# Taylor-softmax attention and an FP6 feed-forward layer on one core: attention in units of two quads by 256 tokens, its rest in 64-row tiles, and the stream normalised on ScalarE

## The reference

```python
x = x + _layernorm(attention(_layernorm(x)))     # x: 16 sequences x 512 tokens x 256
x = x + _layernorm(ffn(_layernorm(x)))
# attention: layer norm with weights, q, k, v of 16 heads of 16; rope on q and k
qk = einsum('bhkd,bhqd->bhkq', q, k) * scale
t = 1.0 + qk + 0.5 * qk * qk
wv = einsum('bhkq,bhqd->bhkd', t / sum(t, -1), v);  return wv @ w_o
# ffn: input and weight rounded to a 6-bit grid in blocks of 32, then x @ w.T + bias
```

## Time and profile before

| | |
|---|---|
| median of 3 runs | 645.59 us (644.71 to 646.18) |
| the profiled execution | 645.33 us, its span 643.7 us |
| PE (TensorE) busy | 615.6 us, 96% |
| VectorE (DVE) busy | 594.8 us, 92% |
| ScalarE (ACT) busy | 530.3 us, 82% |
| GpSimd (POOL) busy | 449.9 us, 70% |
| granted TensorE clock, mean | 0.994 |

### The profile page before, as it was taken

One profiled execution on the slowest core, in us unless ns is written; L12 is line 12 of the kernel. 1 busy time (PEld: TensorE's weight loads), 2 busy tenths in 40 slices (PEclk: granted clock), 3 DMA queues, 4 the chain that ended last, 5 costly groups with the idle time before them and its releaser, 6 DMA issues. The chain is left out here.

```text
span 643.7 us, 20804 instructions
## 1 busy us (share of the span) xinstructions
PE 615.6 (96%) x6660; PEld 459.2 (71%) x6660; DVE 594.8 (92%) x1489; ACT 530.3 (82%) x1448; POOL 449.9 (70%) x785
## 2 busy tenths in 40 slices
PE   8889999899999999999999999999999999999974
PEld 6766667676686777777777777767777766778763
DVE  6999989899899999999999999999999999987796
ACT  4358788788798897989888888978888888999984
POOL 3565476567777778787877777766877777765454
PEclk9999999999999999999999999999999999999997
DMA  7101022222223332332313222223223211230101
GB/s 247 34 3 42 20 78 57 44 68 61 53 74 85 80 81 75 76 87 62 74 53 85 85 72 80 68 58 111 51 71 90 76 39 42 75 85 19 67 27 50
DMA packets 52362, 43.53 MB, mean 68 GB/s; under 512 B 7200, under 2 KB 48544, under 8 KB 52256
## 3 DMA queue, kind: packets, MB, share of 16 engines
q1 hardware_dynamic: 51440, 41.42, 23.9%
q10 hardware_dynamic: 816, 0.79, 0.4%
HBM read 18.65 MB, written 8.39 MB: 42 GB/s over the span
## 5 line engine op out<-in xcount | busy, mean ns | idle before, releaser
L1168 ACT ACTIVATE feat<-ps_f 128x512 f32<-128x512 f32 x256 | 144.5, 599 | 4.9 <-PE ps_f L852 4.3
L691 DVE TENSOR_TENSOR kf<-kf 128x896 f32<-128x896 f32 (+1 forms) x128 | 132.0, 1033 | 1.8
L852 PE MATMUL ps_f<-qT,selr 128*128 128x512 f32 x320 | 122.1, 435 | 1.6 <-ACT qT L1236 1.3
L691 POOL TENSOR_TENSOR kf<-kf 128x224 f32<-128x224 f32 x64 | 76.5, 1195 | 13.3 <-DVE kf L1515 13.0
L1015 PEld LDWEIGHTS ps_mt<-kf,vp 128*32 128x32 f32 x2048 | 63.7, 109 | 29.7 <-issue 28.2
L1015 PE MATMUL ps_mt<-kf,vp 128*32 128x153 f32 x2048 | 79.0, 294 | 0.8 <-DVE kf L691 0.8
L1725 POOL TENSOR_TENSOR qsp<-kf,qsp 128x256 fp32r<-128x256 f32 x64 | 57.8, 903 | 9.8 <-ACT qsp L1259 9.6
L852 PEld LDWEIGHTS ps_f<-qT,selr 128*128 128x128 f32 x320 | 52.8, 190 | 14.9 <-issue 11.0
L913 PE MATMUL ps_o<-feat,main 120*32 120x512 f32 x448 | 59.7, 604 | 0.0
L916 PE MATMUL ps_o<-feat,rm 128*32 128x512 f32 x448 | 58.6, 593 | 0.0
L1737 POOL TENSOR_TENSOR kf<-kf 128x128 f32<-128x128 f32 x64 | 38.2, 596 | 25.6 <-DVE kf L1508 25.5
(11 more groups left out here) (199 smaller groups left out, 1887.4 us busy)
## 6 DMA issues: line engine op xcount, KB each, us to landing
xc<-L_attn_x SPq DMA_DIRECT2D x16, 512.0 KB, 4.5
result<-fin SPq DMA_DIRECT2D x64, 128.0 KB, 2.0
xa<-L_attn_x SPq DMA_DIRECT2D x15, 512.0 KB, 4.3
heads_out<-osb SPq DMA_DIRECT2D x224, 32.0 KB, 2.0
shares<-sums SPq DMA_DIRECT2D x112, 64.0 KB
sums<-osb SPq DMA_DIRECT2D x224, 2.0 KB
wkqv<-L_attn_w_kv ACTq DMA_DIRECT2D x2, 256.0 KB, 4.5
xa<-L_attn_x SPq DMA_DIRECT2D x1, 384.0 KB, 5.8
```

The costliest lines, as they stand in the source:

```text
L691: return eng.tensor_tensor(dims(row, F_MAIN, [[FW, heads], [HD, NR - 1], [1, HD]]), dims(row, F_LIN, [[FW, heads], [0, NR - 1], [1, HD]]), ...
L852: pe.matmul(ps_f[i % 2][:, :], selr[:, i], queries, start=True, stop=True).then_inc(sel_done, 1)
L1168: act.activation(feat[:, p2, i], ps_f[i % 2][:, :], ACT.Square).then_inc(squared, 1)
```

## The change

It has three parts and a new order.

**Units.** In the body a unit is now two quads (p and p+2) by 256 tokens, still 56 of them. Its result goes into two banks: quad p to ps_o, quad p+2 to ps_f[1], so that ps_f[1] is shared with the odd selects. `select_1` and `select_3` wait until the last unit's copy has freed it (f_copied), `attend` until the squares of the odd selects are done. The moving operands of `attend` are 256 columns wide, and there are 16 matmuls in a unit instead of 8. `copy_quad` is two activations of 128x256 in the body instead of one of 128x512. `rm` holds on rows 0 to 63 the rest of quad p and on rows 64 to 127 that of quad p+2; in the second half of `attend` each matmul takes 64 rows and 32 columns, and the two row halves write to different banks. In the last two sequences a unit is still 4 quads by 128 tokens, with the rest in 64-row tiles as well. `fold_kq` puts the columns of w_q in an order to suit (8 matmuls of 2x64 columns and 4 of 256 for 4 of 512, once), and `rest_matrix` and `copy_rest` write the new layout of `rm` with as many instructions as before. `move_quad` has as many DMAs of as many bytes. A unit needs only the queries of its own half of the sequence.

**Normalisation.** `normalise_x` moves from VectorE to ScalarE (z = rs * x + centre_x, scale and bias both read from memory), and POOL gets a new stage `shift_x`, which computes centre_x, 64 of each.

**Order.** All tables of `ORDER` are new (one line of them is shown below); `constant` and `rest_terms` on VectorE are each cut into two stages, and there are 16 idle fills at the start for 10, and 44 idle matmuls for 32 in all.

```diff
-"load_stream": ((0, 1, 6, 11, 20, 32,), (-24,), (76, 87, 98, 108, 119,)),
...
+"load_stream": ((0, 2, 7, 9, 19, 33, 38, 55, 62, 76, 92, 102, 110, 119,), (), ()),
...
-IDLE = {"fill": (4, 4, 4, 4, 4, 6, 6, 7, 7, 9), "drain": ()}
+IDLE = {"fill": (1, 1, 1, 1, 2, 3, 6, 6, 6, 6, 11, 11, 11, 16, 16, 23,), "drain": ()}
...
-rm = sb("rm", [P, 2, NQ, P])
+rm = sb("rm", [P, 2, CH, HQ, VW])
...
+def attend_bank(e):
+
+    return ps_f[1] if e else ps_o
...
+        sp.wait_ge(f_copied, t.n)
         sp.wait_ge(o_copied, t.n)
-        for part in range(NT):
-            sp.dma_start(sums[part * H + HQ * quad:part * H + HQ * (quad + 1)],
-                         osb[HD:P:VW, par, quad, part * P:(part + 1) * P]).then_inc(sums_in, 16)
+        half, p = quad // 2, quad % 2
+        for part in (2 * half, 2 * half + 1):
+            for qd in (p, p + 2):
+                sp.dma_start(sums[part * H + HQ * qd:part * H + HQ * (qd + 1)],
+                             osb[HD:P:VW, par, qd, part * P:(part + 1) * P]).then_inc(sums_in, 16)
         for h in range(HQ):
-            row = HD * (HQ * (quad % 2) + h)
-            sp.dma_start(heads_out[row:row + HD, par, quad // 2], osb[VW * h:VW * h + HD, par, quad]).then_inc(heads_in[par], 16)
+            row = HD * (HQ * p + h)
+            sp.dma_start(heads_out[row:row + HD, par, :, half * 2 * P:(half + 1) * 2 * P],
+                         osb[VW * h:VW * h + HD, par, p:NQ:2, half * 2 * P:(half + 1) * 2 * P]).then_inc(heads_in[par], 16)
...
+    def attend_bank_is_free():
+
+        wait(pe, f_copied, issued["attend"])
...
-            pe.wait_ge(qT_copied, t.n if t.n > BODY else NT * (t.seq + 1))
+            pe.wait_ge(qT_copied, t.n if t.n > BODY else NT * t.seq + 2 * (quad // 2 + 1))
         wait(pe, squared, CHUNKS * n + i - 1 if i else CHUNKS * n)
-        queries = qT[:, par, :, quad * P:(quad + 1) * P] if t.n > BODY else qT[:, par, quad]
+        if i % 2:
+            attend_bank_is_free()
+        half, p = quad // 2, quad % 2
+        queries = (qT[:, par, :, quad * P:(quad + 1) * P] if t.n > BODY
+                   else qT[:, par, 2 * p:2 * p + 2, half * 2 * P:(half + 1) * 2 * P])
         pe.matmul(ps_f[i % 2][:, :], selr[:, i], queries, start=True, stop=True).then_inc(sel_done, 1)
...
+    def feature_bank_is_free():
+
+        if issued["select_1"]:
+            pe.wait_ge(squared, CHUNKS * (issued["select_1"] - 1) + 2)
+        if issued["select_3"]:
+            pe.wait_ge(squared, CHUNKS * (issued["select_3"] - 1) + 4)
...
     def attend(t):
-        par, p2, quad = t.par, t.two, t.tile
-        n = t.n - 1
+        par, p2 = t.par, t.two
+
+        def part(p):
+            return slice(p * P, (p + 1) * P) if t.n > BODY else slice(0, 2 * P)
+
+        def tokens(p, j):
+            g = 2 * p + j // 2
+            return slice(g * P, (g + 1) * P) if t.n > BODY else slice(j // 2 * 2 * P, (j // 2 + 1) * 2 * P)
         wait(pe, o_copied, issued["attend"])
         pe.wait_ge(rm_copied, t.seq + 1)
-        pe.wait_ge(squared, CHUNKS * (n + 1))
-        if t.n > BODY:
-            for qd in range(NQ):
-                part = slice(qd * P, (qd + 1) * P)
-                for h in range(HQ):
-                    pe.matmul(ps_o[VW * h:VW * (h + 1), part], main[0:NP, par, qd, VW * h:VW * (h + 1)], feat[0:NP, p2, h, part],
-                              start=qd == 0, stop=False, skip_group_check=True)
-            for qd in range(NQ):
-                part = slice(qd * P, (qd + 1) * P)
-                for h in range(HQ):
-                    mm = pe.matmul(ps_o[VW * h:VW * (h + 1), part], rm[:, par, qd, VW * h:VW * (h + 1)], feat[:, p2, HQ, part],
-                                   start=False, stop=True, skip_group_check=True)
-            mm.then_inc(quad_done, 1)
-            return
-        for h in range(HQ):
-            pe.matmul(ps_o[VW * h:VW * (h + 1), :], main[0:NP, par, quad, VW * h:VW * (h + 1)], feat[0:NP, p2, h],
-                      start=True, stop=False, skip_group_check=True)
-        for h in range(HQ):
-            mm = pe.matmul(ps_o[VW * h:VW * (h + 1), :], rm[:, par, quad, VW * h:VW * (h + 1)], feat[:, p2, HQ],
-                           start=False, stop=True, skip_group_check=True)
+        pe.wait_ge(squared, CHUNKS * t.n)
+        feature_bank_is_free()
+        pairs = range(CH) if t.n > BODY else [t.tile % 2]
+        for p in pairs:
+            for e in range(2):
+                for j in range(HQ):
+                    pe.matmul(attend_bank(e)[VW * j:VW * (j + 1), part(p)], main[0:NP, par, p + 2 * e, VW * j:VW * (j + 1)],
+                              feat[0:NP, p2, 2 * e + j % 2, tokens(p, j)], start=p == pairs[0], stop=False, skip_group_check=True)
+        for p in pairs:
+            for j in range(HQ):
+                for e in range(2):
+                    rows = slice(e * P // 2, (e + 1) * P // 2)
+                    mm = pe.matmul(attend_bank(e)[VW * j:VW * (j + 1), part(p)], rm[rows, par, p, j],
+                                   feat[rows, p2, HQ, tokens(p, j)], start=False, stop=True, skip_group_check=True)
+                    if p == pairs[-1] and j == HQ - 1 and e == 0:
+                        mm.then_inc(first_done, 1)
...
+    def normalise_x(t):
+        act.wait_ge(x_centred, t.n)
+        wait(act, zT_done, t.n - 2)
+        act.activation(z[:, t.two, 0:D - 1], xa[:, t.par, t.tile, 0:D - 1], ACT.Identity,
+                       bias=centre_x[:, t.two:t.two + 1], scale=rs["x"][:, t.two:t.two + 1]).then_inc(z_ready, 1)
...
+        act.wait_ge(first_done, t.n)
...
+        half, p = quad // 2, quad % 2
         if t.n > BODY:
-            for qd in range(NQ):
-                ins = act.activation(osb[:, par, qd, quad * P:(quad + 1) * P], ps_o[:, qd * P:(qd + 1) * P], ACT.Identity,
+            for qd in (2, 3, 0, 1):
+                ins = act.activation(osb[:, par, qd, quad * P:(quad + 1) * P],
+                                     attend_bank(qd // 2)[:, qd % 2 * P:(qd % 2 + 1) * P], ACT.Identity,
                                      bias=cb[:, par, qd:qd + 1])
+                if qd == 3:
+                    ins.then_inc(f_copied, 1)
             ins.then_inc(o_copied, 1)
             return
-        act.activation(osb[:, par, quad], ps_o[:, :], ACT.Identity, bias=cb[:, par, quad:quad + 1]).then_inc(o_copied, 1)
+        part = slice(half * 2 * P, (half + 1) * 2 * P)
+        act.activation(osb[:, par, p + 2, part], attend_bank(1)[:, 0:2 * P], ACT.Identity,
+                       bias=cb[:, par, p + 2:p + 3]).then_inc(f_copied, 1)
+        act.activation(osb[:, par, p, part], attend_bank(0)[:, 0:2 * P], ACT.Identity,
+                       bias=cb[:, par, p:p + 1]).then_inc(o_copied, 1)
...
+        wait(dve, x_centred, t.n - 2)
         dve.bn_aggr(mv[:, t.two], st[:, t.two]).then_inc(means, 1)
-
-    def normalise_x(t):
-        dve.wait_ge(rstd["x"], t.n)
-        wait(dve, zT_done, t.n - 2)
-        dve.tensor_scalar(z[:, t.two, 0:D - 1], xa[:, t.par, t.tile, 0:D - 1], mv[:, t.two, 0:1], rs["x"][:, t.two:t.two + 1],
-                          ALU.subtract, ALU.mult).then_inc(z_ready, 1)
-
...
+    def sum_linear(t):
+
+        dve.wait_ge(mt_copied, t.seq + 1)
+        wait(dve, cb_ready, t.seq)
+        dve.tensor_reduce(lins[:], mts[:, :, F_LIN:NF], AX.X, ALU.add).then_inc(lins_done, 1)
+
     def constant(t):
-
-        dve.wait_ge(mt_copied, t.seq + 1)
-        dve.tensor_reduce(lins[:], mts[:, :, F_LIN:NF], AX.X, ALU.add).then_inc(lins_done, 1)
         dve.wait_ge(lins_done, t.seq + 1)
...
+    def scale_terms(t):
...
+    def rest_terms(t):
...
+        wait(pool, z_ready, t.n - 2)
         inverse_root("x", t)
+
+    def shift_x(t):
+
+        pool.wait_ge(rstd["x"], t.n)
+        wait(pool, z_ready, t.n - 2)
+        pool.tensor_scalar(centre_x[:, t.two:t.two + 1], mv[:, t.two, 0:1], rs["x"][:, t.two:t.two + 1], -1.0,
+                           ALU.mult, ALU.mult).then_inc(x_centred, 1)
```

541 lines of the change are left out of this document (283 added, 258 removed), and 97 rows, old and new, of the table ORDER.

## The result

The change takes 658.65 us (median of 4 runs, 657.05 to 659.64) against 645.46 for the kernel before (4 runs, 644.71 to 646.18): a ratio of 1.0202, 95% interval 1.0179 to 1.0226. It is 13 us slower; the forecast was 631.5, 14 us faster. The profiled execution has a span of 656.9 us, 13.2 above the 643.7 of before.

What follows compares the result with a forecast made beforehand. PE was taken to set the pace, VectorE just behind. From 645.33 us: -10.0 for 120 to 560 us, -2.8 for the units before, -1.4 for the last units, +0.4 at the start, giving 631.5; range 620 to 642.

Steps and rivals of the forecast that it cites:

- (a): Second half of attend (the rest) on PE: eight 64-row tiles run side by side, 0.87 us becomes 0.435 a unit.
- rival 4: The rest on PE: the two row halves take turns, so it keeps its 0.87 us; 655 us, chance 0.05.
- the 5 foretold: Sign on PE: odd selects' waits for the copy of the shared bank total under 5 us.
- (b): Between the halves of attend on PE: the new change of tile shape adds 0.10 us a unit, bounds 0 and 0.14.
- Rival 2: Shape change within attend on PE: a full drain costs 0.18 us instead of 0.10; 636 us, chance 0.16.
- I give it 10.3 now: PE's gaps from 120 to 560 us: 10.3 us beside 419.7 busy, so the stretch takes 430 instead of 440.
- 411.9 fits into 440: ScalarE from 120 to 560 us: 0.69 us more a unit raises its busy time from 379.43 to 411.9 us.
- rival 3: ScalarE from 120 to 560 us: its in-order waits stay, 40 us of gaps; 653.5 us, chance 0.06.
- The first 120 us: Start of the kernel: a change there of more than 3 us would show the prediction wrong.

Runs made afterwards that it cites:

- The load: Kernel before, plus a 128x128 copy on ScalarE that nobody reads behind each of the 56 unit copies: 3.8 us more; the same was also added to the change.
- copy_vector: The change, with the first of each unit's two copies (from the second bank) on VectorE instead of ScalarE: 675.13 us.
- z_pool_new: The change, with the stream's normalisation on POOL in place of the shift, and four buffers for z: 672.52 us.
- z_pool_old: The kernel before in its own order, with only the stream's normalisation moved from VectorE to POOL: 679.55 us.
- z_old_order: The kernel before, old units and old order, with only the normalisation moved to ScalarE and its shift on POOL: 661.53 us.
- start_list: The change, with the heads of the TensorE, VectorE and POOL lists put nearer to those of the kernel before: 665.51 us.
- shape_price: The change, plus ten rounds each of several mixes of matmul shapes behind the last attend, with no waits: 0.14 to 0.20 us per shape change.

## Why the prediction was wrong

**Right.** PE was the engine with the highest price (0.79 of each us), though not the only bound. The rest takes 0.43 us in eight tiles, as (a) had it: rival 4 is out. The odd selects wait 1.3 us for the copy of their bank by the page, but 4.9 over the whole run when the starts are taken, just under the 5 foretold. The prices of the pieces on ScalarE were near or too high: z 0.52 us from start to start in the mean, the two copies 0.37 each, 0.74 against 0.60 where I added 0.20; its busy time rose by 32 instead of 44 us.

**The shape change (b), mis-sized.** I took 0.10 us for one change, from rows of full size against strips. It is 0.14 into the 64-row tiles and 0.16 out of them: with the changes that fell away 9.0 us in all instead of 6.4. `attend` gives 0.18 a unit instead of 0.31. Rival 2, the drain at 0.18, was near in size but had one change for two. This is some 3 of the 27 us.

**The step that failed: "PE had 5.75 us of gaps ... I give it 10.3 now. This number is chosen, not read."** The page's gaps of PE after are 440 - 428.82 = 11.2, so the number looks well chosen, and is still the wrong quantity. PE's busy time was to fall by 14.3 us over the 46 units and rose by 1.2. `attend` gave 8.2 instead of 14.3, and the same matmuls outside of it took 16.0 us more from start to start, of which 6.5 are gaps and 9.5 lie under the records of the matmuls ahead of them and count as busy. Most of it is waits for ScalarE. PE's gaps must be taken from the starts, against what the same piece takes unheld.

**And behind it the reading of ScalarE's gaps as room.** I asked only whether 411.9 fits into 440. The load shows that 1 us there costs 0.34 even before, and 0.79 with the change. The mechanism is rival 3's, to which I gave 0.06: ScalarE keeps 39.8 us of gaps in the 46 units (40 foretold), VectorE waits 18.9 us for it instead of 1.8, and PE, by the starts, some 11 us instead of 1, while PE's waits for VectorE stay as they were (1.5 and 1.3 us). I forecast rival 3 at 653.5, and 658.65 was measured. Its "against" was that VectorE lives with 18 us of gaps; but ScalarE's list has new work in it on which others wait. Why VectorE's list got by with 18 us of gaps no run shows.

**The sum by the prices.** Taken from start to start and with the means of the prices before and after: ScalarE 33.5 for z and 7.3 for the copies at 0.57 is +23, PE 64 x 0.435 less 9.0 for the shapes and 1.3 for the narrower first half at 0.73 is -13, VectorE 24.9 at 0.57 is -14, POOL +5. That is an estimate, about +1 us: so priced, the change was worth nothing, and some 15 of the 27 us of my error are found. The other 12 us are not settled. In copy_vector, z_pool_new, z_pool_old and z_old_order alike, a step on which others wait cost more than its price when it was moved. 4.1 us lie ahead of the tenth unit, where TensorE runs 4.6 us at a clock of 0.65 behind a wait of 2.2 us; that this is the cause was not shown, since start_list made waits of its own. Nor was an order made anew for the 64-row tiles with z left on VectorE, so what the two parts are worth with an order each is open.

**The first 120 us** "which I have not worked out beyond the units in them": +4.1 us, above the 3 that I named as a sign of error.

## What to carry to other kernels

When several in-order engines are each over 80% busy, gaps are not room: load each engine with a little free work first and see what a microsecond of it costs, then price the change by that. Such a price does not hold for a step that others wait for, and a fixed order tuned around one set of durations has to be made anew with it: here z on ScalarE won 10 us in the order made for it, against a list of VectorE that was not made for z, and cost 17 in the other. Count every change of tile shape on TensorE both ways, and count waits by the starts, not by busy time.

## What the runs showed of the hardware

- A change between full size, strips of 128x32 and tiles of 64x32 costs TensorE 0.14 to 0.20 us in each direction (shape_price). Going from fp32 to fp32r at full size costs nothing that shows: one of each in turn last 0.67 us, alone 0.43 (256 columns, fp32) and 0.23 (512 columns, fp32r).
- Eight 64x32 tiles of fp32 with 256 columns take 0.43 us, as long as four of 128x32 (shape_price). The two row halves wrote to different banks.
- The same normalisation of 128x255 has a mean record of 0.45 us on VectorE before (median 0.41), 0.61 on ScalarE in the change, and 1.42 (z_pool_new) to 1.48 us (z_pool_old) on POOL.
- After a wait of 2.22 us early in the changed kernel, matmuls of 512 columns start 0.43 us apart instead of 0.235; the window 15.8 to 20.4 us has a mean granted clock of 0.65, most of it at 1.2 GHz, and 22.9 to 25.8 us one of 1.00, 2.4 GHz. PE's timeline:

```profile
15.79 0.76 PE L809 MATMUL ps_qk<-wkqv_h,hT_l 128*128 128x512 f32 x1 [2.22 <-DVE wkqv_l L1490]
16.35 0.63 PE L810 MATMUL ps_qk<-wkqv_l,hT_h 128*128 128x512 f32 x1
16.77 0.63 PE L809 MATMUL ps_qk<-wkqv_h,hT_l 128*128 128x512 f32 x1
17.20 0.63 PE L810 MATMUL ps_qk<-wkqv_l,hT_h 128*128 128x512 f32 x1
...
23.76 0.40 PE L809 MATMUL ps_qk<-wkqv_h,hT_l 128*128 128x512 f32 x1
24.00 0.39 PE L810 MATMUL ps_qk<-wkqv_l,hT_h 128*128 128x512 f32 x1
```

- VectorE lost a step of 24.9 us (start to start, 64 times) and its busy time fell by 13.8 only. The 64 products of 128x672 are busy 60.9 us instead of 58.2; why, and where the other 8 us lie, no run shows.
